# Four-layer graph network on one core: adjacency steps kept on chip across two more pass boundaries, squares stored in three passes, and x multiplied by W1 after the first aggregation

## The reference

```python
def reference(x, adj, ...):
    # layer 0
    h = relu(adj @ (f1[:, None] * (adj @ (x @ W1))))
    g = adj @ (f2[:, None] * (adj @ (h @ W2)))
    x = layernorm(x + g)
    # layer 1
    x = layernorm(x + concat([x, adj @ x]) @ W)
    # layer 2
    m = x @ W_msg + b_msg
    gates = sigmoid((m @ W_q) @ (m @ W_k).T / sqrt(128) + gate_bias) * adj * adj
    u = relu(concat([x, gates @ m]) @ W_upd + b_upd)
    x = layernorm(x + layernorm(u) * gamma + beta)
    # layer 3
    s = silu((adj @ x) @ W + b)
    return layernorm(x + silu((adj @ s) @ W + b))
```

## Time and profile before

| | |
|---|---|
| median of 3 runs | 1667.01 us (1663.84 to 1667.1) |
| time of the profiled execution | 1666.21 us |
| its span, first to last instruction | 1664.4 us |
| mean granted PE clock | 0.993 |
| busy: PE, DVE, ACT | 1609.0, 1212.8, 1099.7 us |
| DMA | 484.56 MB, mean 291 GB/s |

### The profile page before, as it was taken

One profiled execution on the slowest core, in us unless ns is written; L12 is line 12 of the kernel. 1 busy time (PEld: TensorE's weight loads), 2 busy tenths in 40 slices (PEclk: granted clock), 3 DMA queues, 4 the chain that ended last, 5 costly groups with the idle time before them and its releaser, 6 DMA issues. The chain is left out here.

```text
span 1664.4 us, 19276 instructions
## 1 busy us (share of the span) xinstructions
PE 1609.0 (97%) x7674; PEld 767.7 (46%) x7674; DVE 1212.8 (73%) x1181; ACT 1099.7 (66%) x784; POOL 54.2 (3%) x49
## 2 busy tenths in 40 slices
PE   7999999999999998999999899999999999999997
PEld 4444444444444444444554444444353444444443
DVE  6866538654766478556899598998989986554886
ACT  5667747764878567755667487796878786454743
POOL 2000000000000000000000000100000100000001
PEclk9999999999999999999999999999999999999999
DMA  9979798979799888996878354554545898764972
GB/s 368 414 301 381 284 419 345 371 284 415 286 388 426 340 317 346 382 340 270 321 283 315 129 202 177 177 207 172 201 166 190 322 371 304 268 250 162 363 276 109
DMA packets 67562, 484.56 MB, mean 291 GB/s; under 512 B 7712, under 2 KB 7872, under 8 KB 9232
## 3 DMA queue, kind: packets, MB, share of 16 engines
q1 hardware_dynamic: 66240, 478.70, 74.6%
q0 software_dynamic: 1088, 4.56, 0.8%
q10 hardware_dynamic: 144, 0.07, 0.0%
HBM read 414.09 MB, written 69.21 MB: 290 GB/s over the span
## 5 line engine op out<-in xcount | busy, mean ns | idle before, releaser
L989 DVE SCALAR_TENSOR_TENSOR a_lo<-a_ring,a_hi 128x2048 f16<-128x2048 f32 x320 | 723.9, 2288 | 301.1 <-ACT a_hi L792 296.9
L792 ACT ACTIVATE a_hi<-a_ring 128x2048 f16<-128x2048 f32 x320 | 604.9, 1905 | 279.4 <-PE spare L594 153.2
L594 PE MATMUL acc<-a_hi,y_hi 128*128 128x512 f16 x1536 | 460.5, 381 | 5.5 <-ACT a_hi L792 3.5
L594 PE MATMUL acc<-a_hi,y_lo 128*128 128x512 f16 x1536 | 460.4, 381 | 0.0
L606 PE MATMUL acc<-a_lo,y_hi 128*128 128x512 f16 x1536 | 406.0, 379 | 7.9 <-DVE a_lo L998 4.9
L606 PEld LDWEIGHTS acc<-a_lo,y_hi 128*128 128x128 f16 x1536 | 149.7, 98 | 192.6 <-DVE a_lo L998 8.1
L594 PEld LDWEIGHTS acc<-a_hi,y_lo 128*128 128x128 f16 x1536 | 150.8, 98 | 182.8 <-issue 2.9
L594 PEld LDWEIGHTS acc<-a_hi,y_hi 128*128 128x128 f16 x1536 | 150.5, 98 | 183.2 <-issue 8.1
L1011 DVE SCALAR_TENSOR_TENSOR gates<-gates,a_ring 128x1024 f32<-128x1024 f32 x128 | 156.1, 1220 | 35.1 <-ACT gates L822 34.8
L805 ACT ACTIVATE a_hi<-gates 128x1024 f16<-128x1024 f32 x128 | 134.8, 1053 | 41.1 <-DVE gates L1011 40.9
L998 DVE TENSOR_TENSOR a_lo<-gates,a_hi 128x1024 f16<-128x1024 f32 x128 | 155.8, 1217 | 0.0
(11 more groups left out here) (119 smaller groups left out, 763.6 us busy)
## 6 DMA issues: line engine op xcount, KB each, us to landing
a_ring<-adj_dram SPq DMA_DIRECT2D x326, 1024.0 KB, 7.4
saved_squares<-squares SPq DMA_DIRECT2D x64, 1024.0 KB, 12.7
a_ring<-saved_squares SPq DMA_DIRECT2D x64, 1024.0 KB, 4.8
x_T<-xt_dram SPq DMA_DIRECT2D x4, 512.0 KB, 8.1
x_rows<-x_dram POOLq DMA_DIRECT2D x1, 2048.0 KB, 12.8
out_dram<-x_rows POOLq DMA_DIRECT2D x3, 512.0 KB, 3.0
out_dram<-x_rows SPq DMA_DIRECT2D x2, 256.0 KB, 2.0
w<-W_dram POOLq DMA_DIRECT2D x2, 64.0 KB, 5.2
```

What stands on the lines that cost most here:

```text
L594: mm = pe.matmul(sums[:, h * BANK:(h + 1) * BANK], blk(y[:, y_pass % 2, :], st.j0 + s), slot(a_hi, st)[:, s, h * BANK:(h + 1) * BANK], sta ...
L792: act.activation(slot(a_hi, st), loaded(st), ACT.Copy, scale=2.0 ** A_EXP).then_inc(s_ahi, 1)
L989: dve.scalar_tensor_tensor(out=slot(a_lo, st).rearrange("p s c -> p (s c)"), in0=loaded(st).rearrange("p s c -> p (s c)"), scalar=2.0 ** A ...
```

## The change

Three things change.

1. `SAVED_IN`: the blocks (2,1) and (3,2) are squared in pass 1 instead of 3; (1,2) and (0,1) in pass 2 instead of 4; (1,1) and (0,0) in pass 3 instead of 4. Steps squared in passes 1 to 4 were 12, 16, 20, 16 and become 20, 24, 20, 0.
2. `KEPT`: three steps of block (1,1) stay on chip from pass 3 to 4 (in the memory of `x_T`, `xn` and `tmp`), three of block (2,3) from pass 4 to 5 (in that of `squares`). They are neither loaded nor split again, and `lead` is bounded around their second uses.
3. Pass 0 has no product on PE: `y_hi` and `y_lo` come from `x` itself, and `project` of pass 1 multiplies by `W1` where it transposed. `xt` is not loaded, `x` is loaded by chunks at the start and not later by POOL.

```diff
-SAVED_IN = {(2, 0): 1, (3, 0): 1, (3, 1): 1, (2, 3): 2, (1, 3): 2, (0, 3): 2, (0, 2): 2, (1, 0): 3, (2, 1): 3,
-            (3, 2): 3, (1, 2): 4, (0, 1): 4, (3, 3): 3, (2, 2): 3, (1, 1): 4, (0, 0): 4}
+SAVED_IN = {(2, 0): 1, (3, 0): 1, (3, 1): 1, (2, 1): 1, (3, 2): 1, (2, 3): 2, (1, 3): 2, (0, 3): 2, (0, 2): 2,
+            (1, 2): 2, (0, 1): 2, (1, 0): 3, (3, 3): 3, (2, 2): 3, (1, 1): 3, (0, 0): 3}
...
-KEPT = [(i, (j * GROUP + t) * SJ) for i, j, t in ((0, 0, 1), (0, 0, 2), (0, 2, 2), (0, 2, 3), (1, 3, 0), (1, 3, 1))]
+IN_SQUARES, IN_X_T, IN_ROWS = RING, RING + SQUARE_SLOTS, RING + SQUARE_SLOTS + 2
+KEPT = {3: dict(zip(kept_steps((1, 1, 1), (1, 1, 2), (1, 1, 3)), (IN_X_T + 1, IN_ROWS, IN_X_T))),
+        4: dict(zip(kept_steps((2, 3, 1), (2, 3, 2), (2, 3, 3)), (IN_SQUARES + 1, IN_SQUARES + 2, IN_SQUARES + 3))),
+        7: dict(zip(kept_steps((0, 0, 1), (0, 0, 2), (0, 2, 2), (0, 2, 3), (1, 3, 0), (1, 3, 1)),
+                    (IN_SQUARES, IN_SQUARES + 1, IN_SQUARES + 2, IN_SQUARES + 3, IN_X_T, IN_X_T + 1)))}
...
             n = LAST_IN_PASS[st.n - RING] + 1 if st.n >= RING else 0
-            return max(n, FIRST_USE[st.n] - RING) if st.p == PASSES else n
+            return max(n, FIRST_USE[st.n] - RING) if any(n <= u < FIRST_USE[st.n] for u in SECOND_USES) else n
...
             for ic in range(NC):
-                sp.dma_start(x_T[:, ic * CH:(ic + 1) * CH], xt[:, ic * CH:(ic + 1) * CH]).then_inc(s_xt[ic], 16)
+                sp.dma_start(x_chunk(0, ic), x[:, ic * CB:(ic + 1) * CB, :]).then_inc(s_x[ic], 16)
                 load(STREAM[ic])
...
-                if p in (1, 3, 4):
+                if p in (3, 4):
                     transposes(lambda b: blk(z_T, b))
...
-                elif p == 0:
-                    by_node((x_T_chunk(p, k), w1[:, :]))
+                elif p == 1:
+                    by_node((z_T, w1[:, :]))
...
             def y_high(p, k):

-                if p in (0, 2, 5):
+                if p == 0:
+                    act.wait_ge(s_x[k], 16)
+                elif p in (2, 5):
                     act.wait_ge(s_rows, nth("rows", p, k, PER_CHUNK["rows"][p] - 1))
...
-            pool.wait_ge(s_alo, STEPS * NC)
-            pool.dma_start(x_rows[:, :, :], x).then_inc(s_x, 16)
```

More of the change, by code:

```diff
@@ L65 @@
 PER_CHUNK = {
[L66 removed]
+    "rows": {1: 1, 2: 1, 3: 1, 4: 2, 5: 5, 6: 1, 7: 1, 8: 1},
     "x_T": {4: 1, 5: 1},
@@ L163 @@
 for _st in STREAM:
-    _keep = _st.p == PASSES - 1 and (_st.i, _st.j0) in KEPT
-    SLOT.append(RING + KEPT.index((_st.i, _st.j0)) if _keep else sum(s < RING for s in SLOT) % RING)
-    HALVES_BEFORE.append(_holds.get(SLOT[-1]))
+    _kept = KEPT.get(_st.p, {})
+    SLOT.append(_kept.get((_st.i, _st.j0), sum(s < RING for s in SLOT) % RING))
+    HALVES_BEFORE.append(_holds.get(SLOT[-1]) if SLOT[-1] < RING else None)
     _holds[SLOT[-1]] = _st.n
@@ L171 @@
 SQUARED_BEFORE = [sum(n < m for n in SQUARED) for m in range(len(STREAM) + 1)]
+SECOND_USES = [n for n, u in enumerate(UNITS) if u.p != u.step.p]
 SAVED = sorted((p, k) for p, k, use in SUM_DONE if use == "next")
@@ L263, in build @@
         s_small = sem("small_loaded")
-        s_w1, s_x = sem("w1_loaded"), sem("x_loaded")
-        s_xt = [sem(f"xt_loaded{i}") for i in range(NC)]
+        s_w1 = sem("w1_loaded")
+        s_x = [sem(f"x_loaded{i}") for i in range(NC)]
         s_a = [sem(f"a_loaded{i}") for i in range(LOADS)]
@@ L350, in halves_free @@
                 eng.wait_ge(used, freed(st))
-            elif n >= RING + SQUARE_SLOTS:
+            elif n >= IN_ROWS:
+                eng.wait_ge(s_wqk_product, 1)
+                eng.wait_ge(s_bias, 2 * BIAS_STEPS)
+            elif n >= IN_X_T and st.p > GATED:
                 eng.wait_ge(s_rows, nth("rows", GATED, NC - 1))
-            elif n >= RING:
+            elif IN_SQUARES <= n < IN_X_T and st.p > GATED:
                 eng.wait_ge(s_lg, NB * NC)
+            elif IN_SQUARES <= n < IN_X_T:
+                for t in range(SQUARE_SLOTS):
+                    eng.wait_ge(s_stored[t], 16 * len(SQUARED) // SQUARE_SLOTS)
         def loaded(st):
@@ L363, in slot @@
                 return t[:, n, :, :]
-            if n < RING + SQUARE_SLOTS:
-                v = squares[:, n - RING, :].bitcast(F16)
-            else:
-                v = x_T[:, (n - RING - SQUARE_SLOTS) * SJ * CH:(n - RING - SQUARE_SLOTS + 1) * SJ * CH].bitcast(F16)
-            at = 0 if t is a_hi else SJ * CH
+            if n < IN_X_T:
+                c = n - IN_SQUARES
+                pair = squares[:, 0:SJ, :] if t is a_hi else squares[:, SJ:2 * SJ, :]
+                return pair.bitcast(F16)[:, :, c * CH:(c + 1) * CH]
+            if n == IN_ROWS:
+                v, at = (xn_T if t is a_hi else tmp_T).bitcast(F16), 0
+            else:
+                v = x_T[:, (n - IN_X_T) * SJ * CH:(n - IN_X_T + 1) * SJ * CH].bitcast(F16)
+                at = 0 if t is a_hi else SJ * CH
             return v[:, at:at + SJ * CH].rearrange("p (s c) -> p s c", s=SJ)
```

28 lines of the change are left out of this document (11 added, 17 removed).

## The result

The changed kernel takes 1674.25 us, the median of five runs (1669.19 to 1674.8), against 1667.01 for the kernel before in the same session: ratio 1.0044, interval 1.0023 to 1.0066. It is slower, by more than the forecast's bound of 0.2%, and 1.2 us above the top of the range. Two later series of runs of the same pair gave 1.0051 (1.0031 to 1.007) and 1.0041 (1.0028 to 1.0054). The profiled execution was the fastest of its five, 1669.19 us, with a span of 1667.3: 3.0 us more than the 1664.4 before, where the medians differ by 7.2.

A forecast was written before the change was run, and what follows sets the result against it. PE, busy 1609.0 of 1664.4 us, was taken as the bound, so only its work and waits count. Terms -8.1 + 3.6 + 11.4 - 5.5 - 2.0 = -0.6 against 1666.21 gave 1665.6 us, no change; range 1656 to 1673.

The forecast's parts named there:

- term 3: Beginning of pass 3: twelve squared units in a row delay ACT and `take_over`; loss 9.7 us plus 1.7 by the clock.
- The start, -8.1: Start: without PE's products of `x_T` by `W1`, unit 6's low products begin at 33.3 instead of 41.42; gain 8.1 us.
- From unit 7 PE needs 2.59 a unit and DVE 2.29, and PE is the bound: Start, behind unit 6: PE, at 2.59 us a unit against DVE's 2.29, sets the pace, within the 8.1 us gain.
- The products, +3.6: Pass 1: products replace transposes on PE, 1.78 us for 0.87 in each of four chunks; loss 3.6 us.
- It is a near thing, with 0 to 2 us in it for that split: Pass 3, split of unit 162: the store that unit 161's square waits for lands just as ACT comes; 0 to 2 us.
- Pass 4, -5.5: Pass 4, unit 232: three fewer DVE splits remove PE's 3.60 us wait for `take_over` and the slow clock; gain 5.5 us.
- Pass 5, -2.0: Pass 5, unit 295: kept steps of units 289 to 291 remove PE's 1.66 us wait for `take_over`; gain 2.0 us.
- three splits fewer on DVE ahead of it: Pass 5, ahead of unit 295's `take_over`: kept steps take 6.9 us of splits off DVE, so the wait goes.
- What is free: Added squares of passes 1 and 2 cost nothing; DMA covers pass 2's 405 GB/s, beside 425 measured, 5% to spare.
- that stores hold squares up: Rival, slower, chance 0.17: DMA does not carry 405 GB/s through passes 1 and 2 and pass 3's twelve squares; 1675 us.
- that pass 4's gain moves: Rival, slower, chance 0.12: `take_over` at unit 232 or 295 waits for something else, gaining 2 instead of 7.5; 1671 us.
- That there is no pile-up: Rival, faster, chance 0.20: ACT gets through pass 3's twelve squares with a PE wait of 4 us or less; 1658 us.

The follow-up runs named there:

- the first trace: Profiled execution of the changed kernel in its first series, no further edit: 1669.19 us, span 1667.3 us, against 1664.4 for the kernel before.
- the third trace: Profile of the changed kernel run a third time, no edit: span 1671.4 us; median 1673.46 us, ratio 1.0041 to the kernel before.
- ACT's work alone: Kernel before, with the eight steps of (1,1) and (0,0) squared once more in pass 3 into scratch memory, not stored: 1678.78 us, ratio 1.0079.
- the three kernels that square fewer steps in pass 3: Changed kernel with (0,0) squared in pass 4, ratio 1.001; (1,0) in pass 1, 1.0018; (0,0) and (0,1) in pass 4, 1.0011; without pass-4-to-5 kept steps where (0,0) moved.
- squares alone: Kernel before with the new `SAVED_IN` table and nothing else: 1687.2 us, ratio 1.0128 to the kernel before.
- part 3 alone: Changed kernel with the squares and kept steps of the kernel before, so only `x` split itself and `W1` in pass 1: 1663.78 us, ratio 0.9987.

## Why the prediction was wrong

The forecast was no change, 1665.6 us, and the step that failed most is the size of the stores' part of term 3, 3.3 us too small. The sum was -0.6 against the profiled execution of before; by its terms:

1. *The start, -8.1.* Right in place and size up to unit 6 (33.3 forecast, 32.94 in the trace). Then the faster start meets the loads, which the step "From unit 7 PE needs 2.59 a unit and DVE 2.29, and PE is the bound" left out. Unit 6 on PE, and ACT's waits for its loads behind it, in the changed kernel:

```profile
32.94 1.04 PE L622 MATMUL acc<-a_lo,y_hi 128*128 128x512 f16 x4 [0.57 <-DVE a_lo L1004]
...
39.75 1.91 ACT L809 ACTIVATE a_hi<-a_ring 128x2048 f16<-128x2048 f32 x1 [2.44 <-DMA a_ring<-adj_dram]
43.70 1.91 ACT L809 ACTIVATE a_hi<-a_ring 128x2048 f16<-128x2048 f32 x1 [2.04 <-DMA a_ring<-adj_dram]
```

That gives 2.1 us back. The term is -6.4. Here, too, DMA moved less than the forecast's 425 GB/s at a full share: 269 GB/s from 35 to 40, at 1.04.

2. *The products, +3.6.* Right: 3.65.

3. *Pass 3, +11.4.* The mechanism was right, and the part that is ACT's as well: 11.9 with no added store. Mis-sized was the sentence "It is a near thing, with 0 to 2 us in it for that split". Up to the split of unit 162 three squares waited 0.97, 1.20 and 1.18 us, 3.35 in all, and PE's wait was 9.9 for the 7.7 foreseen. DMA gives 2 MiB each 4.90 us, and ACT asks at 3.60: from the square of unit 159 on every one waits. That steady pace is the forecast's own (4.93). What it left out is that DMA did not hold 425 GB/s up to there: 342 and 380 GB/s from 420 to 440, worth 3.0 us by the estimate above, which is nearly the 3.35. No run changes this rate, and why it falls at a full share stays open. Term: +14.7.

4. *Pass 4, -5.5.* Right: -6.0, with the order of waits as described. 5.3 of it is at unit 232, the wait of 3.60 and 1.7 by the clock (the sum had 1.9), and 0.6 at unit 228, which the sum did not have.

5. *Pass 5, -2.0.* The step "three splits fewer on DVE ahead of it" failed. DVE was idle there, and the chain began at PE's transposes of the same epilogue. The wait is 1.66 as it was. I had read how many splits stood in the queue, and not whether the queue was full.

6. *What is free.* Cover by DMA held in pass 2: the table has no loss of PE between units 98 and 157. The Trainium skill, "DMA: Bandwidth & Descriptors", section "Where 436 GB/s comes from", has the HBM side bind at about 358 GB/s for such transfers; as a ceiling the trace doesn't agree, with 424 to 431 GB/s in windows that mix loads and stores. The Trainium skill ties the 358 to both cores of an HBM domain streaming, and has 425 GB/s for 16 MB by one core alone (same page, section "Measured (HBM→SBUF, 128 partitions, SWDGE, issued from GpSimd)"). This kernel runs on one core, and its windows of 424 to 431 agree with that. A loss of 0.7 at unit 98 was not foreseen; it is in the first trace and not in the third.

Together: -0.6, and 3.3 (pass 3), 2.1 less 0.4 (start), 0.7 (unit 98), 2.0 (pass 5), -0.5 (pass 4) and 0.4 (all else) make 7.0, about what the third trace (7.0) and the medians (7.2) show. In the first trace two stretches of low clock did not come and one wait was shorter, 4.1 us in all by chance, which is why it is only 3.0 over.

The chances do not add up as written. Slower by more than 0.2% are two rivals, 0.17 and 0.12, and 0.04 of the forecast, 0.33 together; faster are 0.20 and 0.05, 0.25 together. The text gives 0.28 for each.

Of the rivals, that stores hold squares up came true, but in pass 3 and not in passes 1 and 2, where I had put its price. The rival that pass 4's gain moves did not happen there; 2.0 of its 5.5 us came in pass 5. That there is no pile-up is refuted. What is shown: ACT's part of term 3, by the run with ACT's work alone, and that the stores add to it, by the waits of the squares in the traces and by the three kernels that square fewer steps in pass 3. Argued only: that the dip of DMA's rate from 420 to 440 is what made the stores' part larger than forecast, and that the load of `x` by POOL made the loss at unit 98 with squares alone. Open: why DMA moves less at a full share in some stretches, and why a wait of some 2 us brings a low clock in one execution and not in another.

## What to carry to other kernels

Work moved out of a stage where it is hidden must be put beside the pace of the stage where it lands, engine by engine and then for DMA: taking one away mostly uncovered the other (a wait of 8.6 us for 9.9, and 10.8 us lost for 14.7). A rate read in one full window is not that of every full window: here 425 GB/s was the price, and 342 to 380 was paid where it mattered. In engines that keep a written order, first ask whether the late instruction can stand further up; here an earlier `take_over` in four places took 9 us off by the ratios (0.9987 to 0.9931), while the new places of the squares and the kept steps together made the kernel slower (0.9987 to 1.0044). And before counting what is taken away ahead of a wait, look whether the waiting queue had an idle gap there: if so, its chain begins somewhere else.

## What the runs showed of the hardware

A store and a load of 1 MiB each, together, took 4.90 us in steady state (half of 458.14 less 448.34), 428 GB/s, beside 425 in the earlier trace rows. A DMA share near 1 did not always mean that rate: the changed kernel has 342 GB/s at 1.01 in 420 to 430 and 269 at 1.04 in 35 to 40. Around waits of PE of 7 to 10 us the half clock lasted 10.2 us in five of the traces and 13.7 in one, around waits of 5 to 6 us 6.8 in two; around waits under 4 us it was mostly 3.4. Whether one followed the wait of 2.12 us at unit 320 varied between two executions of the changed kernel, at 1.65 us; behind the wait of 3.6 us at unit 232 it came in the kernel before and not with part 3 alone, at 1.7.
